# A new order of the first step in a fused dense-convolution kernel: four convolution groups of the second pair of images run earlier, and the engines' order around them follows

## The reference, cut to what matters

```python
x1 = relu(conv2d(x, w1, b1, 2, 2))                                  # 3x3, dilation 2
x2 = relu(conv2d(concatenate((x, x1), 1), w2, b2, 2, 2))
x3 = relu(conv2d(concatenate((x, x1, x2), 1), w3, b3, 2, 2))
x4 = relu(conv2d(concatenate((x, x1, x2, x3), 1), w4, b4, 2, 2))
fea = relu(concatenate((x, x1, x2, x3, x4), 1))
fea = einsum('ij,bcjk,lk->bcil', H, fea, H)
out = conv2d(fea, w6, b6, 1, 1) + x
```

## Time and profile before

| | |
|---|---|
| median of 3 runs | 377.47 us (377.09, 377.47, 379.12) |
| the profiled execution, its own time | 378.54 us |
| span of the profile, first to last instruction | 376.7 us |
| mean granted TensorE clock | 0.995 of full speed |
| busy in the span | PE 96%, DVE 75%, ACT 62%, POOL 3% |

### The profile page before, as it was taken

How to read it: one execution, slowest core, us unless ns; L and a number is a source line. 1 busy time by engine, 2 the same in 40 slices (tenths; PEclk the granted TensorE clock), 3 DMA queues, 4 the chain that set the end, 5 groups by cost and what they waited for, 6 DMA issues and landing times.

```text
span 376.7 us, 7714 instructions
## 1 busy us (share of the span) xinstructions
PE 361.7 (96%) x2847; PEld 270.4 (72%) x2852; DVE 281.3 (75%) x528; ACT 232.7 (62%) x380; POOL 12.1 (3%) x17
## 2 busy tenths in 40 slices
PE   8979999999999999999999999999999897899986
PEld 7868878797697869787987879697866342466633
DVE  4847687937965894789479658936897699677986
ACT  5435838645953684387459546842877795277871
POOL 2000000030030001000000000000110000000000
PEclk9989999999999999999999999999999999999999
DMA  7746336224531433352244315133400000000005
GB/s 242 226 89 170 96 78 162 52 53 117 137 85 45 117 107 82 78 145 55 68 108 142 75 46 123 49 84 77 105 2 3 0 1 0 2 4 2 2 29 197
DMA packets 19678, 30.67 MB, mean 81 GB/s; under 512 B 4544, under 2 KB 11840, under 8 KB 19648
## 3 DMA queue, kind: packets, MB, share of 16 engines
q1 hardware_dynamic: 19008, 29.35, 29.5%
q10 hardware_dynamic: 640, 0.92, 1.1%
HBM read 10.86 MB, written 2.10 MB: 34 GB/s over the span
## 4 chain that ended last, share of the span: by engine, by line
PE 78%; DVE 9%; DMA 4%; ACT 3%; issue 3%; SPq 2%; DVEq 0%; ACTq 0%
PE sums_ps L779 24%; PE mix_ps L881 12%; PE ps L1423 9%; PE mix_ps L910 6%; PE sums_ps L837 5%; DMA D<-D 4%; PE mix_ps L885 4%; PE mix_ps L837 4%; PE ps L1475 3%; PE ps L1382 3%; PE ps L1365 2%; DVE part L509 1%; PE mix_ps L919 1%; PE mix_ps L821 1%; SPq L251 1%
## 5 line engine op out<-in xcount | busy, mean ns | idle before, releaser
L779 PE MATMUL sums_ps<-D,w_hl 128*128 128x480 f32 (+1 forms) x504 | 118.0, 388 | 1.3 <-DMA D<-D 1.2
L779 PEld LDWEIGHTS sums_ps<-D,w_hl 128*128 128x128 f32 x504 | 93.3, 188 | 27.3 <-issue 5.4
L881 PE MATMUL mix_ps<-mix_hl,F_hl 128*128 128x288 f32 x360 | 64.3, 296 | 0.7 <-ACT Y L403 0.7
L403 ACT ACTIVATE Y<-mix_ps 128x288 f32<-128x288 f32 x120 | 48.9, 410 | 21.6 <-PE mix_ps L885 9.7
L881 PEld LDWEIGHTS mix_ps<-mix_hl,F_hl 128*128 128x128 f32 x360 | 55.3, 190 | 2.6 <-ACT Y L403 1.4
L341 ACT ACTIVATE r<-sums_ps,bias_sb 64x512 f32<-64x512 f32 x28 | 19.1, 682 | 41.9 <-PE sums_ps L779 41.8
L509 DVE TENSOR_TENSOR part<-mix_ps,part 64x512 f32<-64x512 f32 x16 | 11.1, 693 | 36.3 <-PE mix_ps L837 36.1
L885 PE MATMUL mix_ps<-mix_hl,X 96*128 96x288 f32 x120 | 35.2, 298 | 0.0
L1423 PE MATMUL ps<-q_q,diag 64*64 64x512 bf16 x576 | 33.4, 388 | 0.6 <-DVE q_q L1230 0.6
L1100 ACT ACTIVATE q_I<-ps,w_bias 128x1024 f32 x20 | 21.2, 1110 | 15.8 <-PE ps L1423 15.8
L1423 PEld LDWEIGHTS ps<-q_q,diag 64*64 64x64 bf16 x576 | 20.8, 105 | 13.1 <-issue 1.3
(11 more groups left out here) (145 smaller groups left out, 492.6 us busy)
## 6 DMA issues: line engine op xcount, KB each, us to landing
D<-D SPq DMA_DIRECT2D x88, 112.0 KB, 2.3
x_own<-in_x_pads SPq DMA_DIRECT2D x16, 256.0 KB, 3.2
F<-r SPq DMA_DIRECT2D x64, 64.0 KB, 2.0
F<-in_x_mix SPq DMA_DIRECT2D x16, 128.0 KB, 2.4
F<-part SPq DMA_DIRECT2D x32, 64.0 KB, 2.0
xb<-in_x_res SPq DMA_DIRECT2D x8, 256.0 KB, 2.7
out<-q_res SPq DMA_DIRECT2D x7, 256.0 KB, 2.1
w_raw<-in_w_conv SPq DMA_DIRECT2D x6, 192.0 KB, 3.6
```

Of the source, the lines that this page charges most:

```text
L403: nc.scalar.activation(Y[:, u, g], banks(p, u)[:, g % 4, 0:MIX], ACT.Copy).then_inc(y_out, 1)
L779: last = nc.tensor.matmul(tap_out(conv_sums(s, u)[:, bank, :], d), w_hl[:, wp, n, d, :], tap_in(D[f][u][:, xp], d), start=start and d == 1 ...
L881: nc.tensor.matmul(y, F_hl[u][:, xp, h, k], mix_hl[:, wp], start=n == 0, stop=False, skip_group_check=True)
```

## The change

All of it is in step 0 and at the head of step 1.

- TensorE: `conv0(1,0)` moves ahead of `conv2(0,0)`; `conv0(1,1)` and `conv0_on(1,0)` follow `conv2(0,1)`, then `turn_peaks`, `conv3(0,0)`, `spread_weights`, `conv3(0,1)`. Step 1 begins with the wait for `scales_ready` and `conv0_on(1,1)`; `conv0_on(1,0)` is no longer there. `conv0_on` of pair 1 waits for `added[u]` to be 1. `turn_peaks` uses bank 3 in place of bank 1. The two waits ahead of `mix(0,0)` stay.
- ScalarE: `high_x(1, ...)` moves from behind the second `high_2` to ahead of the first. The end of the step becomes `high_f(0,0)`, `relu(1,1,0)`, `high_4(0,0)`, `copy_4(0)`, `relu(1,1,1)`, `high_f(0,1)`, `high_4(0,1)`, `copy_4(1)`.
- VectorE: the twelve pad memsets leave it. `low_x(1,1,0)` takes the place of the four of x2. `weight_peaks` is cut in two: the first reduction stays ahead of `split(0,3,1)`, the other two follow it. The end of the step becomes `low_f(0,0)`, `split(1,1,0)`, `add_parts(0,4,0)`, `weight_scales`, `low_4(0,0)`, `split(1,1,1)`, `add_parts(0,4,1)`, `low_f(0,1)`, `low_4(0,1)`.
- GpSimd: the pad memsets of all three features, linked by a semaphore, as its first work.

```diff
@@ gpsimd
+            def clear_pads(f):
+                for u in range(2):
+                    n = 4 * (f - 1) + 2 * u
+                    flat = D[f][u][:].bitcast(F32).rearrange("p h a n -> p h (a n)")
+                    if n:
+                        pool.wait_ge(zeroed, n)
+                    nc.gpsimd.memset(flat[HALO_M2:HALO_M2 + 32, :, 0:HALO], 0.0).then_inc(zeroed, 1)
+                    pool.wait_ge(zeroed, n + 1)
+                    nc.gpsimd.memset(flat[HALO_P4:HALO_P4 + 32, :, DSZ - HALO:DSZ], 0.0).then_inc(zeroed, 1)
+
+            for f in range(1, 4):
+                clear_pads(f)
+            pool.wait_ge(zeroed, 12)
             nc.gpsimd.memset(keep.magic[:], IN_BF16).then_inc(keep.made, 1)
@@ scalar
                     high_mix()
+                    high_x(1, 1, 1)
...
-                if not no_next(s):
+                if not no_next(s) and not is_first(s):
                     high_x(s + 1, 1 - odd, batch + 2)
...
-                for u in range(2):
-                    high_f(s, u)
-                    if is_first(s):
-                        relu(1, 1, u)
-                high_4(s, 0)
-                copy_4(0)
+                high_f(s, 0)
+                if is_first(s):
+                    relu(1, 1, 0)
+                    high_4(0, 0)
+                    copy_4(0)
+                    relu(1, 1, 1)
+                    high_f(0, 1)
+                else:
+                    high_f(s, 1)
+                    high_4(s, 0)
+                    copy_4(0)
                 high_4(s, 1)
@@ vector
-            def weight_peaks():
+            def first_weight_peak():
                 w = w_raw[:].rearrange("p n m -> p (n m)")
                 dve.wait_ge(int_in, 16)
                 nc.vector.tensor_reduce(stat[:, 0:1], w[:, 0:W1], AX.X, ALU.max, apply_absolute_value=True)
+
+            def other_weight_peaks():
+                w = w_raw[:].rearrange("p n m -> p (n m)")
                 nc.vector.tensor_reduce(stat[:, 1:2], w[:, WX:W2], AX.X, ALU.max, apply_absolute_value=True)
...
-            clear_pads(1)
             low_w(0)
...
-                    dve.wait_ge(zeroed, 2)
+                    dve.wait_ge(zeroed, 4)
...
                     low_mix()
-                    clear_pads(2)
+                    low_x(1, 1, 0)
                 add_parts(s, 2, 0)
                 if is_first(s):
-                    dve.wait_ge(zeroed, 4)
+                    dve.wait_ge(zeroed, 8)
...
                 if not no_next(s):
-                    low_x(s + 1, 1 - odd, 0)
+                    if not is_first(s):
+                        low_x(s + 1, 1 - odd, 0)
                     low_x(s + 1, 1 - odd, 1)
...
-                    clear_pads(3)
-                    dve.wait_ge(zeroed, 6)
+                    dve.wait_ge(zeroed, 12)
...
                 split(s, 3, 0)
                 if is_first(s):
-                    weight_peaks()
+                    first_weight_peak()
                 split(s, 3, 1)
                 if is_first(s):
+                    other_weight_peaks()
                     top_weights()
...
                 add_parts(s, 4, 0)
                 if is_first(s):
                     weight_scales()
+                    low_4(0, 0)
+                    split(1, 1, 1)
+                    add_parts(0, 4, 1)
+                    low_f(0, 1)
                 else:
                     low_f(s, 0)
-                add_parts(s, 4, 1)
-                low_4(s, 0)
-                low_f(s, 1)
-                if is_first(s):
-                    split(1, 1, 1)
-                else:
+                    add_parts(s, 4, 1)
+                    low_4(s, 0)
+                    low_f(s, 1)
                     turn_s1(p, 0)
@@ tensor
             def conv0_on(s, u):
                 weights(s, 2)
+                if is_second(s):
+                    pe.wait_ge(added[u], 1)
                 conv(s, u, 0, 1, 1, True).then_inc(x_used[u], 1)
...
                     if is_second(s):
-                        conv0_on(1, 0)
                         pe.wait_ge(scales_ready, 1)
                         conv0_on(1, 1)
                         transform_ready()
...
                 conv1(s, 0)
                 conv1(s, 1)
+                if is_first(s):
+                    conv0(1, 0)
...
                 conv2(s, 0)
                 conv2(s, 1)
                 if is_first(s):
-                    conv0(1, 0)
+                    conv0(1, 1)
+                    conv0_on(1, 0)
                     turn_peaks()
-                    conv0(1, 1)
-                    spread_weights()
...
                 conv3(s, 0)
+                if is_first(s):
+                    spread_weights()
                 conv3(s, 1)
```

More of the change, by code:

```diff
@@ L618, in top_weights @@
                 dve.wait_ge(id_in, 16)
-                link(nc.vector.tensor_reduce(top[:], sums_ps[0:3, 1, 0:NP], AX.X, ALU.max))
+                link(nc.vector.tensor_reduce(top[:], sums_ps[0:3, 3, 0:NP], AX.X, ALU.max))
                 nc.vector.tensor_scalar(top_d[:], ident[0:3, 0:3], top[:], None, ALU.mult).then_inc(top_ready, 1)
@@ L650, in sum_weights @@
                 last.then_inc(w_quantised, 1)
-            def clear_pads(f):
-                for u in range(2):
-                    flat = D[f][u][:].bitcast(F32).rearrange("p h a n -> p h (a n)")
-                    nc.vector.memset(flat[HALO_M2:HALO_M2 + 32, :, 0:HALO], 0.0)
-                    nc.vector.memset(flat[HALO_P4:HALO_P4 + 32, :, DSZ - HALO:DSZ], 0.0).then_inc(zeroed, 1)
             def low_w(n):
@@ L790, in turn_peaks @@
                 pe.wait_ge(stat_ready, 1)
-                pe.wait_ge(added[0], 1)
-                nc.tensor.transpose(sums_ps[0:3, 1, 0:NP], stat[:], ident[:]).then_inc(stat_turned, 1)
+                pe.wait_ge(added[1], 1)
+                nc.tensor.transpose(sums_ps[0:3, 3, 0:NP], stat[:], ident[:]).then_inc(stat_turned, 1)
             def spread_weights():
                 pe.wait_ge(top_ready, 1)
-                pe.wait_ge(added[1], 1)
                 nc.tensor.matmul(sums_ps[:, 3, HALF - 3:HALF], ones[0:3, :], top_d[:], start=True, stop=True)\
```

## The result

The changed kernel takes 385.63 us in the median of six runs (384.49 to 387.48), the kernel before 378.58 in six runs: ratio 1.0199 [1.0174, 1.0224]. It is slower, as forecast, but by 7.05 us, and 385.63 lies outside the range. The profiled execution took 385.23, 6.69 more than that of before; its span is 383.4, 6.7 more. The difference of the two profiles is therefore a fair picture of the whole.

The account below looks back on a forecast made before the run. TensorE, busy 96% of the span, was taken as the bound, with a ScalarE and VectorE chain ending nearly together at 42 us. Profiled 378.54 plus 2.6 gave 381.1, less half of 1.07: 380.6 us, range 378.4 to 382.2, about 0.8.

Parts of the forecast that it names:

- if the faster runs are without: Step 0 before the change: runs lacking the clock fall at 23 us lose 1.15 us more and end at the same place.
- The memsets on GpSimd: Pads in step 0: forecast at nothing; rival, GpSimd's memset stops VectorE, up to 1.8 us more, 380.6 to 382.4, chance 0.04.
- The sum: Whole kernel: 378.54 + 2.6 = 381.1, less half of 1.07, gives 380.6; TensorE's work from 42.53 us on taken as unchanged.
- The clock in the mix: `mix(0,0)`: loss of 2.12 us without a clock fall, 3.0 with one; the middle, 2.6, was taken.
- The case with the fall: `mix(0,0)`: a clock fall costs 1.7 us among its 32 products, so they end 3.0 us later, at 47.8.
- The halo of x2: Ahead of `conv2` in step 0: halo lands at 22.53 us as before, so `conv2` still starts at 22.57.
- Carries through: Rival: the 3.78 us given back in step 0 are kept to the end, 374.8 us; chance 0.08.
- Absorbed later: Rival: TensorE's further waits of 1.2 and 0.6 us give back 1.8 us, 378.8 us; chance 0.14.
- The clock stays down through all of the mix: Rival: low clock in both gaps and all of `mix(0,0)`, which ends 5.8 us later, 384.3 us; chance 0.04.

Follow-up runs that it names:

- 1: Changed kernel with the old order at the end of step 0 on ScalarE and VectorE: 379.17 us, ratio 1.0060 to the kernel before.
- 2: Kernel before with only the new order at the end of step 0 on ScalarE and VectorE: 382.60 us, ratio 1.0121.
- 4: Changed kernel with 3 and 6 unread products of ones in TensorE's two new waits: 383.81 us, ratio 1.0170 to the kernel before.
- 12: Kernel of 5 with ScalarE's second copy of x4 for image 1 moved into step 1: 378.99 us, ratio 1.0024 to the kernel before.
- 13: Kernel of 12 with only 4 of the fill's 9 products ahead of `conv2`, 5 behind: 378.63 us, ratio 1.0024 to the kernel before.
- 11: Changed kernel with four more idle products in a TensorE wait of the quantised block: 384.54 us, ratio 1.0172 to the kernel before.
- 7: Kernel before with 18 unread products of ones ahead of `mix(0,0)`, TensorE kept busy: 380.72 us, ratio 1.0049.
- 3: Changed kernel with `conv0_on(1,0)` back at the head of step 1, ahead of the `scales_ready` wait: 386.07 us, ratio 1.0217 to the kernel before.
- 8: Changed kernel with twelve tiny products replacing four of eight warm-up products, instruction stream 8 further on: 386.39 us, ratio 1.0215 to the kernel before.
- 9: Changed kernel with 16 tiny products behind its 8 warm-up products, moving the instruction load earlier: 386.26 us in two runs, ratio 1.0221 to the kernel before.
- 6: Kernel before with only the pads on GpSimd, the early x and the split peaks: 379.46 us, ratio 1.0035.
- 14: Kernel before with only ScalarE's second copy of x4 for image 1 moved later, no fill: 378.71 us, ratio 1.0004.
- 5: Changed kernel with the old ScalarE and VectorE order and `conv0_on(1,0)` back in step 1, fill kept: 379.31 us, ratio 1.0036 to the kernel before.
- 10: Kernel of 6 with 10 tiny products in the place of the fill, ahead of the halo wait: 379.23 us, ratio 1.0021 to the kernel before.

## Why the prediction was wrong in size

**What held.** Direction and mechanism: the gap at 20.5 us closes, the fall there is gone, TensorE waits for the scales and then for `added[1]`, and the new order on VectorE and ScalarE sets that time. Experiments 1 and 2 show the order as the main cost, 4 gives 2.20 us for it at the full clock (forecast 2.12). That "if the faster runs are without" the fall at 23 us they end about 1.15 lower held too: beside experiments 12 and 13 the kernel before ran 23 times, 12 times at a mean clock of 0.999 or more (median 377.5) and 11 times below (378.7). The memsets on GpSimd collided with nothing. The Trainium skill's rule on a shared port (SBUF — State Buffer, "Who interferes with whom") was not tried by this: the memsets end at 6.2 us, and the first cast in VectorE's rows stands at 7.40.

**The step that failed is the premise under "The sum": that what TensorE has left to do from 42.53 on "is the same in both kernels", and so costs nothing more.** It cost 2.86 us: 0.86, 1.33 and 0.67 in the list above. Up to the end of the mix the forecast had 2.6 and 3.84 came; with 3.84 in its place the forecast's own sum gives 381.8, inside the range. The pieces, with what each was forecast at:

- *The quantised block*, 1.33, forecast at nothing. The program there is the same; the clock was not. Experiment 11 gets 0.94 of it back with products in TensorE's wait there; 7 shows that lateness alone does not bring the fall. The prediction took 1.2 and 0.6 for the longest waits behind step 0. The view that the earlier trace rows are from lists others in this block, and the fall came behind the second of these:

```profile
PE ps L1351 <- DVE q_sc L1153: 1.0, 2, 0.5
PE ps L1351 <- DVE q_c_most L1205: 0.9, 1, 0.9
```

  Why the clock falls there in some kernels is open: in the fifteen profiles after the change and of the experiments it fell in seven, all with the new order or without the cover (the changed kernel, 1 to 4, 8, 9), and in none of the other eight, which but for 11 all have the old order and the cover. In 1 and 2 the wait ahead of it was 0.85, as before, so its length does not decide.
- *VectorE's longer idle time* (the other 0.4 of the block) *and the 0.67 at the end*, forecast at nothing. These do not scatter. The idle time ahead of the fold is 0.49 and the end 3.01 to 3.03 us in the six profiles that have the programs of the changed kernel on VectorE and ScalarE (the changed kernel, 3, 4, 8, 9, 11); in the other ten it is 0.10, and the end 2.34 to 2.54. So some 1.0 us goes with those two programs, in places where their instructions are the same as before. The cause is open.
- *Later halo waits*, 0.86, forecast at nothing. These scatter. Between the same two instructions, at 113 and 163 us in the kernel before, the fifteen profiles gained or lost against that of before anything from -0.6 to +2.1 us, with the same program there; the changed kernel, with +1.0, stands near the middle, and the profile of before low. They were not separated from chance, and experiment 6's and 14's small losses are of this size.
- *The clock in the mix*, "I take the middle, 2.6". The lone group behind the mix is 3.84 late; less the late halo, 0.63, that is 3.21. The case with the fall, priced at 3.0, was the right one; the middle was a choice without a row for it. The clock fell at 37.08, in the nine products after the wait of 1.92, and again at 43.92, 1.3 us into the mix. The first fall was not forecast and cost nothing: it only shortened the wait behind it, to 2.24 where the forecast had 3.4. Experiment 4 shows that both falls go with TensorE's idleness, and what is left without them.
- *The halo of x2*, 0.63, forecast at nothing: "it is issued no earlier, so `conv2` still starts at 22.57". It was issued no later either, and landed later. What was missed is a transfer that no line of the program issues: TensorE's instructions. In the five profiles with no product ahead of the wait for the halo (before, 2, 6, 7, 14) the next load came at 23.3 to 24.4, when `conv2` was running, and the halo took 3.48 to 4.06 us from its last issue. With products ahead of that wait, even 4 or 10 tiny ones, the load came at 19.0 to 21.2, on the transfer, and the halo took 4.65 to 5.26 in all ten (the changed kernel, 1, 3 to 5, 8, 10 to 13).

**The rivals.** "Carries through" fell by its own condition: `added[1]` was counted at 42.27, not before 38. Experiments 5 and 12 tried what is left of it, without the waits: 1.0036 and 1.0024. About 0.5 to 0.9 us of the fill goes to the late halo (`conv2` at 23.07 in 5 and 12, 23.45 in 13), and what TensorE is ahead after that is given back at group 4, or in later halo waits. "Absorbed later" had the wrong sign in the changed kernel, where more loss came later; 1.2 us of 3.8 came back in experiment 7, which is within the scatter of the halo waits. "The clock stays down through all of the mix" did not happen in the profile of the changed kernel, where it was back at 47.3 us; in those of 8 and 11 it was down until 49.5 and 48.5. The range lacked the case that came: a fall of the clock in a stage whose program is unchanged, which cost 0.94.

## What to carry to other kernels

Before an engine's idle time is filled, look for the engine that ends next: here the order on two other engines gave back, and more, what the gap had offered. Price a new wait of TensorE with the fall of the clock behind it, and do not put the stages behind the change at nothing because their program is the same: look there too at the waits that TensorE already has. Here a fall followed one of 0.85 to 1.25 us in seven profiles of fifteen. Work put ahead of a wait also moves the engine's instruction loads: look in the DMA view whether one of them now meets a transfer that is waited for.

## What the runs showed of the hardware

- One load of 16,384 bytes of TensorE's instructions, on a queue of its own, went with a halo's last stretch that was some 1.2 us longer (the middle of 4.65 to 5.26 in ten profiles against that of 3.48 to 4.06 in the five without it). Experiment 10 moved the load alone: 5.01, where 6 had 3.54.
- The clock fell to 1.2 GHz after a wait of TensorE of 1.92 us, and not at the same place after one of 1.26 us with products of ones ahead of it (experiment 4). The length of the wait alone does not decide: ahead of `conv2` one of 2.12 brought a fall before, and one of 2.08 in experiment 13, with four products in front of it, none. In experiment 9 the wait for the scales was 1.92 too, and the nine products behind it ran at the full clock:

```profile
38.85 2.28 PE L796 MATMUL sums_ps<-D,w_hl 128*128 128x512 f32 x9 [1.92 <-DVE inv L649]
```

- GpSimd's memset of 32 x 128 numbers took 0.20 us, close to VectorE's 0.17 in the earlier trace rows and far from the bound of 1.80 in the earlier trace rows.
